# A fused attention and feed-forward kernel on eight cores: other block sizes for the down projection, and a last block cut in pieces

## What is computed

```python
x = x + layernorm(attn(layernorm(x)))
x = x + layernorm(ffn(layernorm(x)))

# attn, on Z = [X (256 rows); Y (the rest)]
att = relu((B @ X).T @ (C @ X)); att[-1, -1] = 0
X_out = X + A @ (X @ att);  Y_out = Y + r * (Y @ att)

# ffn, INTER = 5632, ternary weights, one scale per output
g = (x @ gate_w.T) * gate_s;  u = (x @ up_w.T) * up_s
out = ((silu(g) * u) @ down_w.T) * down_s
```

## Time and profile before

| | us |
|---|---|
| median of 3 runs | 1046.83 (1046.16 to 1047.46) |
| profiled execution, device time | 1047.22 |
| its span, slowest core (6) | 1045.7 |
| spans of the eight cores | 1041.7 to 1045.7 |
| mean granted TensorE clock | 0.990 to 0.993 of full speed |
| VectorE busy | 590.6 (56% of the span) |
| ScalarE busy | 289.0 (28%) |
| transfers on GpSimd's queue | 75.77 MB in 43.9% of 16 engines' span |
| transfers on the hardware queues | 24.50 MB in 6.9% |

### The profile page before, as it was taken

How to read it: one execution, slowest core, us unless ns; L and a number is a source line. 1 busy time by engine, 2 the same in 40 slices (tenths; PEclk the granted TensorE clock), 3 DMA queues, 4 the chain that set the end, 5 groups by cost and what they waited for, 6 DMA issues and landing times.

```text
span 1045.7 us, 12874 instructions; the slowest of 8 cores (1041.7 to 1045.7 us)
## 1 busy us (share of the span) xinstructions
PE 1007.7 (96%) x4797; PEld 465.4 (45%) x4893; DVE 590.6 (56%) x814; ACT 289.0 (28%) x427; POOL 52.6 (5%) x99
## 2 busy tenths in 40 slices
PE   6999999999999999999999999999999999999993
PEld 2445444444444444444444444444444444444441
DVE  4755666644654655555555555555554655554576
ACT  3645676622111111112112111111121111112266
POOL 0000000110001001001000010010010010001010
PEclk8999999999999999999999999999999999999997
DMA  8503331768326527428329229238248247339489
GB/s 234 113 1 121 121 122 81 139 110 134 61 41 105 97 41 118 84 41 133 69 41 154 48 46 156 41 61 141 41 71 131 43 82 118 57 65 166 116 126 196
DMA packets 18348, 101.09 MB, mean 97 GB/s; under 512 B 2160, under 2 KB 2288, under 8 KB 9456
## 3 DMA queue, kind: packets, MB, share of 16 engines
q0 software_dynamic: 13680, 75.77, 43.9%
q1 hardware_dynamic: 4608, 24.50, 6.9%
HBM read 152.95 MB, written 16.78 MB: 162 GB/s over the span
## 4 chain that ended last, share of the span: by engine, by line
PE 86%; DMA 4%; DVE 3%; ACT 3%; issue 2%; POOL 0%; DVEq 0%; ACTq 0%; POOLq 0%
PE ps L822 45%; PE ps L860 28%; PE ps L455 5%; DMA dwb<-dw 3%; PE ps L424 3%; PE ps L755 3%; DMA bcb<-bc 1%; DVE xr L520 1%; ACT lc L480 1%; PE ps L373 1%; DVE acc L849 1%; ACT lc L557 0%; ACT pc L345 0%; PE ps L404 0%; DMA xr<-xtop 0%
## 5 line engine op out<-in xcount | busy, mean ns | idle before, releaser
L822 PE MATMUL ps<-bop,wr 128*128 128x512 bf16 x2299 | 516.4, 379 | 2.8
L822 PEld LDWEIGHTS ps<-bop,wr 128*128 128x128 bf16 x2352 | 230.0, 98 | 277.4 <-issue 0.3
L860 PE MATMUL ps<-dwb,hdn 128*128 128x512 bf16 x1322 | 305.4, 379 | 2.2 <-DMA dwb<-dw 0.9
L875 DVE TENSOR_TENSOR acc<-acc,ps 128x2048 f32<-128x2048 f32 x70 | 160.2, 2288 | 213.6 <-PE ps L860 213.6
L860 PEld LDWEIGHTS ps<-dwb,hdn 128*128 128x128 bf16 x1344 | 131.2, 98 | 160.6 <-issue 3.2
L795 ACT COPY tmp<-ps 128x512 f32<-128x512 f32 x126 | 73.3, 582 | 347.9 <-PE ps L822 347.9
L803 DVE TENSOR_TENSOR tmp<-tmp,ps 128x512 f32<-128x512 f32 x126 | 86.5, 686 | 93.0 <-ACT tmp L795 46.5
L455 PE MATMUL ps<-att,xT 128*128 128x512 bf16 x497 | 116.4, 379 | 1.2 <-DVE xT L352 0.3
L782 DVE TENSOR_TENSOR wr<-wr 128x1024 bf16<-128x1024 bf16 x168 | 114.2, 686 | 4.7 <-DMA wr<-gu 0.2
L733 ACT ACTIVATE sg<-tmp,cpks 128x512 bf16<-128x512 f32 x63 | 45.5, 722 | 237.1 <-DVE tmp L803 237.1
L455 PEld LDWEIGHTS ps<-att,xT 128*128 128x128 bf16 x512 | 49.2, 98 | 57.3 <-issue 1.3
(11 more groups left out here) (96 smaller groups left out, 405.7 us busy)
## 6 DMA issues: line engine op xcount, KB each, us to landing
wr<-gu POOLq DMA_DIRECT2D x44, 1024.0 KB, 10.2
dwb<-dw POOLq DMA_DIRECT2D x42, 512.0 KB, 17.7
xr<-x SPq DMA_DIRECT2D x8, 1024.0 KB, 6.5
y<-xr SPq DMA_DIRECT2D x8, 1024.0 KB, 3.9
y<-acc POOLq DMA_DIRECT2D x6, 1024.0 KB, 9.0
xr<-xtop SPq DMA_DIRECT2D x4, 512.0 KB, 9.0
x1r<-y SPq DMA_DIRECT2D x2, 1024.0 KB, 7.0
dsB<-dsr SPq DMA_DIRECT2D x1, 1024.0 KB, 12.9
```

The lines of the kernel that those rows point to most:

```text
L822: t = pg.pe(lambda e, c=c: e.matmul(ps[:, bk, :], wr[:, m % WS, ws, c * P:(c + 1) * P], bop[:, bs, c, :], start=(k in (1, 2, 5) and c == 0 ...
L860: t = pg.pe(lambda e, gi=gi, li=li, hc=hc: e.matmul(ps[:, banks[hc], :], hdn[:, gi % HS, tt * P:(tt + 1) * P], dw_at(gi)[:, hc * MQ:(hc + ...
L875: acc_t[tt] = pg.dv(lambda e: e.tensor_tensor(dst, dst, src, ALU.add), [t, acc_t[tt]])
```

## The change

Six edits.

1. The block sizes become 6, seven times 4, and 10. Nine blocks where ten were.
2. Block 0's eight down steps go to n = 0, 1, 2 of block 1 as 3, 3, 2, its fourth iteration has none; other blocks keep 0, 3, 3, 2. Where an iteration has two steps, the second moves ahead of `product(m, 4)`. The loads behind block 0 are six down tiles and come at n = 2.
3. Late down tiles: 36 and 37 are issued at m = 39, 38 and 39 at m = 40, 40 to 42 at m = 41 (in `dwx`), 43 at m = 42 (in `dwy`), each over freed weight slots; `hdx` and `hdy` hold the two last hidden tiles. The load of down_s moves from m = 41 to m = 42.
4. In the last block row tiles 3, 4 and 5 are worked in two halves, 6 in a half and two quarters, 7 in quarters.
5. Row tiles 4 to 7 get x1 from a reloaded copy by an addition on VectorE and a plain transfer in two halves (7: four quarters); only 0 to 3 use accumulating transfers.
6. The small arithmetic for mean and variance moves from VectorE to GpSimd (row tiles 0 to 6) and to ScalarE (the sum of the squares' parts, the variance inside Ln's bias and scale, the bias for the normalisation).

```diff
-BLKS = [4] * 9 + [8]
+BLKS = [6] + [4] * 7 + [10]
...
     def dw_at(gi):
-        return {IT - 2: dwx0, IT - 1: dwx1}.get(gi, dwb[:, gi % DS, :])
+        if gi == IT - 1:
+            return dwy
+        return dwx[:, gi - (IT - 4), :] if gi >= IT - 4 else dwb[:, gi % DS, :]
...
-        n_d = (0, 3, 3, 2)[n] if 0 < b and n < 4 else 0
-        done = (0, 0, 3, 6, 8)[min(n, 4)]
+        plan = (3, 3, 2, 0) if b == 1 else (0, 3, 3, 2)
+        n_d = plan[n] if 0 < b and n < 4 else 0
+        done = sum(plan[:n])
...
-            if n_d == 3:
+            if n_d:
                 down(b - 1, done + 1)
...
-            if n_d:
-                down(b - 1, done + n_d - 1)
+            if n_d == 3:
+                down(b - 1, done + 2)
...
-        if b > 0 and n == 3:
+        if b > 0 and n == (2 if b == 1 else 3):
             for li in range(BLKS[b - 1]):
                 gi = BASE[b - 1] + li + DS
                 if gi < BASE[-1] + 2:
                     load_dw(gi, [hd_last[gi - DS]])
-        if m == NM - 4:
-            for gi in range(BASE[-1] + 2, IT - 2):
+        if m in (NM - 5, NM - 4):
+            for gi in range(2 * m - 42, 2 * m - 40):
                 load_dw(gi, [hd_last[gi - DS]])
         if m == NM - 3:
-            load_dw(IT - 2, [w_free[NM - 3]])
-            ds_ld = pg.dma("sync", "dsb", dsB[:, :], t_ds.ap(),
-                           [w_free[NM - 3]])
+            for gi in range(IT - 4, IT - 1):
+                load_dw(gi, [w_free[NM - 3]])
         if m == NM - 2:
             load_dw(IT - 1, [w_free[NM - 2]])
+            ds_ld = pg.dma("sync", "dsb", dsB[:, :], t_ds.ap(),
+                           [w_free[NM - 2]])
...
-    x1_at = {6: 0, 7: 1}
+    x1_at = {4: 0, 5: 1, 6: 2, 7: 3}
...
+    def rstd(tt):
+        c = slice(tt, tt + 1)
+        n = len(PIECES.get(tt, (0,)))
+        a = mq_t[tt]
+        for k in range(n - 1 if tt < LAST else 0):
+            a = pg.ac(lambda e, k=k: e.activation(
+                vw[:, c], qpart[:, tt, k:k + 1], AF.Identity, scale=1.0 / D,
+                bias=vw[:, c]), [a, sq_t[(tt, k)]])
...
+    two, four = ((0, 1), (2, 3)), ((0, 0), (1, 1), (2, 2), (3, 3))
+    PIECES = {3: two, 4: two, 5: two, 6: ((0, 1), (2, 2), (3, 3)), 7: four}
...
+        taken(tt, 0)
+        summed(tt, 0)
+        taken(tt, 1)
+        rstd(tt - 1)
+        if tt < LAST:
+            normed(tt - 1)
+            summed(tt, 1)
+            for j in range(2, len(PIECES[tt])):
+                taken(tt, j)
+                summed(tt, j)
+            joined(tt)
+            if tt - 1 not in x1_at:
+                add_up(tt - 1)
+            else:
+                store(tt - 1, 0, R)
+                store(tt - 1, R, D)
+    tt = LAST
+    normed(tt - 1)
+    summed(tt, 1)
+    taken(tt, 2)
+    summed(tt, 2)
+    store(tt - 1, 0, R)
+    taken(tt, 3)
+    summed(tt, 3)
+    joined_last(tt)
+    rstd(tt)
+    store(tt - 1, R, D)
+    for k in range(4):
+        normed(tt, k * MQ, (k + 1) * MQ)
+        store(tt, k * MQ, (k + 1) * MQ)
```

More of the change, by code:

```diff
@@ L736, in silu, with hd_at @@
         return sl_t[q]
+    def hd_at(gi):
+        return {IT - 2: hdx, IT - 1: hdy}.get(gi, hdn[:, gi % HS, :])
     def gated(gi, h, q, src, after):
@@ L845, in build_nc, with acc_part @@
     part_t = {}
[L847 to L851, removed]
+    def acc_part(tt, ks, banks, name):
+        src = ps[:, banks[0]:banks[-1] + 1, :].rearrange("p a b -> p (a b)")
+        acc_t[(tt, name)] = pg.dv(lambda e: e.tensor_tensor(
+            acc[:, tt, ks], acc[:, tt, ks], src, ALU.add),
+            [part_t[banks[-1] % 4], acc_t[tt]])
+        for bk in banks:
+            tok_bank[bk] = (acc_t[(tt, name)],)
     def down_mm(b, tt, banks, order, sig):
@@ L980, in build_nc @@
     t = down_mm(b, 0, (0, 1, 2, 3),
-                [(li, hc) for li in range(6) for hc in range(4)], never)
+                [(li, hc) for li in range(8) for hc in range(4)], never)
     product(NM - 1, 4)
@@ new lines, in cols, with taken, summed @@
+    def cols(tt, j):
+        lo, hi = PIECES[tt][j]
+        return slice(lo * MQ, (hi + 1) * MQ)
+    def taken(tt, j):
+        lo, hi = PIECES[tt][j]
+        acc_part(tt, cols(tt, j),
+                 [4 * (tt % 2) + k for k in range(lo, hi + 1)], j)
+    def summed(tt, j):
+        scaled(tt, cols(tt, j), wpart[:, tt, j:j + 1], j)
+        q = (qlast[:, :] if (tt, j) == (LAST, 3) else
+             qpart[:, tt, j:j + 1])
+        squares(tt, cols(tt, j), q, j)
+    eps_q = pg.dv(lambda e: e.memset(qpart[:, LAST, 3:4], EPS * D))
@@ L1077, in build_nc @@
     junk_t = [None]
[L1078 removed]
+    for tt in range(DT):
+        banks = (0, 1, 2, 3) if tt % 2 == 0 else (4, 5, 6, 7)
         if tt > 0:
[L1080 to L1093 removed]
@@ L1117, in build_nc @@
-    part(tt, 0)
-    joined_sq(tt - 1)
-    variance(tt - 1)
-    rstd(tt - 1)
-    part(tt, 1)
-    bias(tt - 1)
-    normed(tt - 1)
-    part(tt, 2)
-    part(tt, 3)
-    store(tt - 1, 0, R, nrm_t[(tt - 1, None)], "y0")
-    joined(tt)
-    joined_sq(tt)
-    variance(tt)
+            ends_at = [hi for lo, hi in PIECES.get(tt, ())]
+            t = down_mm(b, tt, banks, by_bank,
+                        lambda li, hc: hc in ends_at and li == BLKS[b] - 1)
+        if tt not in PIECES:
+            if tt > 0:
+                acc_add(b, tt, banks, t)
+                rstd(tt - 1)
+            whole(tt)
+            if tt > 0:
+                normed(tt - 1)
+                add_up(tt - 1)
+            continue
```

191 lines of the change are left out of this document (85 added, 106 removed).

## The result

The changed kernel takes 1053.87 us (median, 1053.67 to 1054.10) against 1047.06 us for the kernel before (four executions, three of them those of the table ahead): the ratio is 1.0066, with a 95% interval of 1.0054 to 1.0078. It is 6.8 us slower. The forecast was 1051.0 with a range of its own of 1049 to 1053, and slower had 57%; the measured time lies above that range and inside the wide one, which reached to 1054.5. The slowest core is now core 1, with a span of 1052.5 us in place of 1045.7.

What follows compares the result with a forecast made beforehand. TensorE, busy 96% of the 1045.7 us span, was taken as the bound; 1047.2 + 5.3 (first boundary) - 1.1 (tail) = 1051.4 us, 1051.0 for the median. Range 1049 to 1053, wide range 1044.4 to 1054.5.

Steps and rivals of the forecast that it cites:

- part 2: First block boundary: two more down weights delay tile 12's load, so TensorE loses 5.3 us in gaps of 3.1 and 2.2.
- The landing: Tile 12's weight load after block 0: behind two more down weights at 3.05 us each, it lands at X + 35.5.
- X: Issue time of the first load in the burst at block 0's end; 319.69 us in the kernel before.
- TensorE's arrival: Iteration of m = 11: without a stall, TensorE would reach the second down step at X + 34.2.
- The clock: Rival at the first boundary: the 3.1 us gap drops TensorE's clock, costing 2 us more, 1053.0 us; chance 12%.
- the stall: TensorE's wait at the first boundary for tile 12 and VectorE's add behind it: 5.3 us, bounds nothing and 9.8.
- No wait for down weights longer than now: Sign for the changed trace: at the next block boundaries, waits for down weights get no longer than before.
- part 3: Late loads of down tiles 36 to 43 and the scale: covered before first use, 0 us.
- T: End of the last matmul; 1028.76 us in the profiled kernel before.
- The tail: Time after the last matmul: 0.4 us gained in VectorE's chain, 0.7 in quarter stores; 1.1 in all, bounds 0 and 3.6.
- The chain through VectorE and ScalarE: Last block: one row tile of 5 and 6 takes 9.7 us against 8.6 of matmuls; last normalisation at T + 8.7.
- The rival of a shorter tail: Tile 6's normalisation never holds VectorE and quarters land in 2.6 us: 3.6 us gained; with the stall 1048.5 us, 10%.

Runs made afterwards that it cites:

- filled kernel: Changed kernel plus 14 matmuls, results never read, before tile 12's first product: 1051.51 us, ratio 1.0049; repeated 1052.53 us, ratio 1.0065.
- run without the stall: Changed kernel with down tiles 10 and 11 issued one iteration later, behind tile 12's weight load: 1046.75 us, ratio 1.0005.

## Why the prediction was right, and where it was off

**The place and the mechanism** of part 2 were right: tile 12, in the iteration of m = 11, a combination at the head of VectorE's queue, two gaps of TensorE with a product between. The two runs with moved tiles show it by taking it away in two steps: one tile moved leaves 2.8 us of the 6.8, two leave 0.5. That the sum is off by no more than 2.6 us is in part luck: the errors below add up to 4.7 us on one side, and 2.1 us of scatter between two cores stand on the other.

**The landing was mis-sized.** I had X + 35.5 by two tiles at 3.05 us. Tile 12 landed at X + 12.1 + 25.0 = 37.1 on core 1, and X + 34.7 to 37.3 over the cores. The 3.05 us came from what lay between the first landing and the fourth down tile's. The whole burst gives another rate: before, 4.19 MB were written from about X + 2.8, when the first bytes came, to X + 29.4, 158 GB/s or 3.3 us a tile, so X + 36.1. That the rest, up to 1 us, varies from core to core and run to run is seen, its cause not. With 37.1 the same working gives 37.1 + 0.2 + 1.48 + 2.29 - 34.2 = 6.9 us.

**TensorE's arrival was placed too late.** I had X + 34.2 for the down step, from a row of the chain of waits and one short iteration. The run with two tiles moved has it at X + 33.8 to 33.9. On core 1 the step began at 384.51 = X + 41.0, so it was 7.2 us late, and with the 0.65 us of the slow clock in it these are the whole 7.9 us of the stretch; no other wait stands there.

**The clock** was a rival with 12% and 2 us. It did fall, at gaps of 2.6 us and more, on all cores of the profiled run, and on core 1 it cost the 0.65 us by which the step at 384.51 is longer (4.27 against 3.62). The rival was right in its event and wrong in its price: 0.65 us here, 2 us on two cores with shorter gaps, nothing on three with gaps of 4.4 to 5.2 us, nothing measurable in the kernel's time. The measured 1053.9 us lies nearer to this rival's 1053.0 than to the forecast's 1051.0, but not for its reason: the stall itself was larger. By the rule that I cited from the Trainium skill, TensorE: Matmul & The Clock Gate (Why this matters for your kernels), the rate had to fall, and the trace agrees (0.76 over 378 to 380, then 0.50). That the price hides in a wait which follows is what the comparison with the filled kernel showed.

**Later boundaries.** "No wait for down weights longer than now" was wrong for core 1: 0.8, 0.7 and 0.3 us against at most 0.5. The run without the stall has such waits too. What makes them, and why on some cores only, was not tested.

**The late loads** (part 3) cost nothing, as forecast: from tile 41's load to T all cores took 125.50 or 125.51 us, two short iterations (24.17 us) and 101.33 us behind them, and TensorE has no gap there.

**The tail.** The chain through VectorE and ScalarE was right and nearly to size: tile 6's first add at T - 11.6 (forecast T - 11.8), tile 7's at T - 1.8 (T - 2.1), the period 9.84 us (9.7). From there each link was a little longer, 6.45 us for 6.2 to the end of tile 6's normalisation and 1.16 for 1.05 in the last small steps, and the last normalisation began at T + 9.4 and not T + 8.7. The quarter stores landed in 3.4 us, not 3.0. So the 1.1 us of gain became a loss of 0.15. The rival of a shorter tail named the right wait, which did not go by itself; it bounded its worth too low: with the sums moved the mean tail is 12.8 us, 4.6 less than before, and I had 3.6, though the quarter stores landed in 3.8 to 5.4 us there and not in the 2.6 of that bound.

**The sum.** Forecast +5.3 - 1.1 = +4.2 (1051.4 for the profiled execution); measured +6.8. The differences: landing +1.5, TensorE's earlier arrival +0.4, clock +0.65, tail +1.25, later waits +0.9 (2.6 against 1.7), the start of core 1's loop against core 6's -2.1; in all +2.6. The last is scatter between cores that a forecast from one core cannot give.

**What I did not see.** I costed the new part against the old one as they stood, each with its own block size. The chance lay in the corner between them: the longer block with the old order of VectorE, which waits for no normalisation. Some 4 us lay there (3.6 measured), and the chain of 9.7 against 8.6 us, which stands in the forecast, pointed at them.

## What to carry to other kernels

When a burst of loads grows, count the bytes from the first issue to the load that is needed next, divide by the rate of the whole burst and not of its middle, and then ask what stands behind that load on the in-order engine that waits for it: here a wait of 3.1 us for the landing became a loss of 5.3 in the working, and one of 5.1 became 7.2 in fact. A post-processing step that waits for another engine belongs one row tile later in its engine's order; the same additions made the tail nearly 5 us longer in one place than in the other. Two parts that each pay for the other's room must be timed in all four combinations.

## What the runs showed of the hardware

The granted clock fell at gaps of 2.63 to 5.23 us and stayed up at those of 2.17 us and less, among them two of 1.8 us with a 1.9 us product between. It fell 2.2 to 4.7 us behind the end of the last matmul ahead of the gap, on some cores only when matmuls ran again, and stayed down for 3.4 us on some cores and 6.8 on others (its mean over the 16 us from 374 to 390 was 0.89 or 0.79). The work slowed in that time cost nothing as long as a wait behind it was longer than the slowing; what decides between the two lengths is open.

GpSimd's small sums on 128 x 1 took 0.19 to 0.22 us each (two on core 1 about 1.0), 0.35 us from one dependent start to the next, against 0.9 us for the issue of an accumulating transfer on the same engine, and hid entirely.

The accumulating transfers of 1 MB took 8 to 12 us from issue to landing. The four quarter stores at the end landed in 2.2 to 2.6 us in the run with tiles 4 and 5 accumulated, in 3.1 to 4.0 in the changed kernel; in 3.6 to 5.0 in the kernel before; and in 3.8 to 5.4 in the run with the sums moved. With the old last part and the new blocks the tail was 12.2 to 13.0 us on four cores, whose quarter stores landed in 2.9 to 3.8 us, and 14.2 to 14.7 on the four others, where they took 4.9 to 5.2, with the last normalisation at T + 5.3 on all of them. What slows the stores is open; the run with the fastest of them has as many accumulating transfers as the kernel before, and its six last stores are issued over 7.6 us, against 4.3 us in the one that only moves tile 6's first sum.
